# Local attention on one Trainium2 core: the mask written by eight small products instead of two full-size ones

## The reference, cut to what matters

```python
DEPTH, HEADS, DIM_HEAD, WINDOW, QK_SCALE = 6, 16, 64, 32, 8.0
def local_attention(q, k, v):          # b, h, n=128, d=64
    nw = n // WINDOW                   # 4 blocks of 32 queries
    bq, bk, bv = (t.reshape(b, h, nw, WINDOW, d) for t in (q, k, v))
    def look(t):                       # keys: the block before, and the own block
        p = jnp.pad(t, ((0, 0), (0, 0), (1, 0), (0, 0), (0, 0)))
        return jnp.concatenate([p[:, :, :nw], p[:, :, 1:]], axis=3)
    bk2, bv2 = look(bk), look(bv)      # 64 keys for each block
    mask = (it < jb) | (it > jb + WINDOW) | (jb == -1)
    sim = jnp.einsum('bhwie,bhwje->bhwij', bq, bk2) * QK_SCALE
    sim = jnp.where(mask, -jnp.finfo(sim.dtype).max, sim)
    attn = jax.nn.softmax(sim, -1)
    return jnp.einsum('bhwij,bhwje->bhwie', attn, bv2)
```

## Time and profile before

| | |
|---|---|
| median of 3 runs | 2673.61 us (2669.58 to 2676.61) |
| the profiled execution: its time | 2672.38 us |
| its span | 2670.5 us |
| busy: PE | 2441.2 us, 91% |
| busy: DVE, ACT, POOL | 79%, 71%, 67% |
| granted clock of PE, mean of the span | 0.989 |

### The profile page before, as it was taken

One profiled execution on the slowest core, in us unless ns is written; L12 is line 12 of the kernel. 1 busy time (PEld: TensorE's weight loads), 2 busy tenths in 40 slices (PEclk: granted clock), 3 DMA queues, 4 the chain that ended last, 5 costly groups with the idle time before them and its releaser, 6 DMA issues.

```text
span 2670.5 us, 98096 instructions
## 1 busy us (share of the span) xinstructions
PE 2441.2 (91%) x36165; PEld 1693.3 (63%) x36169; DVE 2098.9 (79%) x4531; ACT 1896.1 (71%) x6651; POOL 1781.0 (67%) x1605
## 2 busy tenths in 40 slices
PE   6989877778999999999999999999999999889999
PEld 3656644446666666666666666666666666558884
DVE  6777789987888888888888888888888888665544
ACT  3666688867787778878877887887788878543323
POOL 1566787649878778777778787787777777512210
PEclk8999999999999999999999999999999999989999
DMA  5000020021111211121112111121112111100000
GB/s 138 11 10 11 11 49 13 12 66 33 34 31 39 56 40 32 31 64 40 32 32 55 40 40 32 45 52 40 31 33 63 40 33 32 40 1 1 1 1 16
DMA packets 177424, 92.28 MB, mean 35 GB/s; under 512 B 40950, under 2 KB 173256, under 8 KB 176976
## 3 DMA queue, kind: packets, MB, share of 16 engines
q1 hardware_dynamic: 168352, 82.00, 12.0%
q0 software_dynamic: 8192, 4.21, 1.2%
q10 hardware_dynamic: 432, 0.07, 0.0%
HBM read 32.06 MB, written 3.76 MB: 13 GB/s over the span
## 4 chain that ended last, share of the span: by engine, by line
POOL 34%; PE 21%; issue 11%; DVE 7%; ACT 3%; DMA 1%; SPq 1%; DVEq 0%; POOLq 0%; ACTq 0%
POOL rs L1505 16%; POOL t_pair L1495 12%; POOL pr L1486 5%; PE bank L1113 2%; PE scores L1158 2%; PE bank L1169 2%; PE bank L1106 1%; PE bank L1797 1%; PE bank L1821 1%; ACT pr L1428 1%; PE scores L1140 1%; PE bank L1198 1%; PE bank L2054 1%; DMA rg_prod<-vt 1%; PE bank L1791 1%
## 5 line engine op out<-in xcount | busy, mean ns | idle before, releaser
L1505 POOL TENSOR_TENSOR rs<-ssc,neg_half 128x8 f32<-128x8 f32 x384 | 645.9, 1682 | 30.4 <-DVE ssc L1376 30.4
L1495 POOL TENSOR_TENSOR t_pair<-qn_pair,tabs 128x512 f32<-128x512 f32 x384 | 488.7, 1273 | 12.7 <-DVE qn_pair L1360 9.9
L1428 ACT ACTIVATE pr<-scores,negmax 128x64 f32<-128x64 f32 x1536 | 462.1, 317 | 3.9
L1486 POOL TENSOR_TENSOR pr<-pr,rec 128x256 f32<-128x256 f32 x384 | 235.1, 612 | 333.2 <-DVE rec L1353 333.2
L1106 PE MATMUL bank<-wqk,xs 128*128 128x512 f32 x768 | 396.0, 598 | 4.8 <-DVE qn_pair L1360 3.6
L1422 ACT COPY vt<-bank 128x256 f32<-128x256 f32 x361 | 134.4, 372 | 281.2 <-PE bank L1169 243.8
L1428 ACT ACTIVATION_READ_ACCUMULATOR pr<-scores,negmax 128x1 f32 x1536 | 321.1, 209 | 0.0
L1011 POOL DMA_INDIRECT rg_win<-rg_images,share_down x256 | 259.6, 1014 | 83.4 <-issue 55.5
L1113 PEld LDWEIGHTS bank<-ident,qr_pair 128*128 128x128 f32 x1536 | 180.2, 142 | 180.2 <-DVE qr_pair L1340 143.2
L1360 DVE TENSOR_TENSOR qn_pair<-bank,rs 128x512 f32<-128x512 f32 x384 | 260.5, 678 | 20.0 <-POOL rs L1505 19.7
L1340 DVE TENSOR_TENSOR qr_pair<-t_pair 128x512 f32<-128x512 f32 x384 | 264.8, 690 | 10.7 <-issue 0.7
(11 more groups left out here) (309 smaller groups left out, 5505.4 us busy)
## 6 DMA issues: line engine op xcount, KB each, us to landing
rg_prod<-vt SPq DMA_DIRECT2D x1536, 32.0 KB
wqk<-in_L_ffn_Wqkv SPq DMA_DIRECT2D x20, 256.0 KB, 2.8
rg_win<-rg_images,share_down POOLq DMA_INDIRECT x256
wv<-in_L_ffn_Wqkv SPq DMA_DIRECT2D x20, 128.0 KB, 2.8
wo<-in_L_ffn_Wo SPq DMA_DIRECT2D x20, 128.0 KB
w<-in_L_ffn_W SPq DMA_DIRECT2D x6, 341.0 KB
rg_images<-rg_prod SPq DMA_DIRECT2D x1, 1625.0 KB, 7.9
rg_images<-XT SPq DMA_DIRECT2D x16, 64.0 KB, 1.5
```

Of the source, the lines that this page charges most:

```text
L1428: ex = act.activation(pr[t % 2][:, h * BAND:(h + 1) * BAND], sl_ps[:, h // 2, h % 2 * BAND:(h % 2 + 1) * BAND], ACT.Exp, bias=negmax[t % 2 ...
L1486: pool.tensor_tensor(p, p, over(rec[t % 2][:, :], [P, GH, BAND], 2), ALU.mult).then_inc(a.p_scaled, 1)
L1495: pool.tensor_tensor(t2[t % 2][:, :].rearrange("p (i h f e) -> p i h f e", i=2, h=GH, f=2), qn[t % 2][:, :].rearrange("p (i h f e) -> p i ...
L1505: pool.tensor_tensor(rs[t % 2][:, :], ssc[t % 2][:, :], neg_half[:, 0:8], ALU.pow)\
```

## The change

The mask is written in the tile shape of the scores: for each block of 32 queries and each half `r` of the rows one product, eight in all, each 64 rows by 32 columns with 128 moving columns. The operands change places. The stationary one is now a 64x32 piece of the mask, which is stored transposed (keys down, queries across) and twice, once for each half of the rows; the moving one is the 64x64 diagonal block of `ident16`, read twice for the two heads. A tile's mask has the same 32 rows and 128 columns of PSUM as its scores.

```diff
@@ build @@
-        local_mask = sb("local_mask", [P, BAND], BF16)
+        local_mask = sb("local_mask", [P, P], BF16)
...
-        mask_wide, pick_wide = t1[0][:, 0:BAND], oT[1][0:ME, 0:ME * P]
+        mask_wide, pick_wide = t1[0][:, 0:P], oT[1][0:ME, 0:ME * P]
@@ score @@
-                for r in range(2):
-                    pe.matmul(sl_ps[:, r, :].rearrange("p (a k) -> p a k", a=2), ident16[:, :],
-                              over(local_mask[:, :], [P, 2, BAND], 1), start=True, stop=False, skip_group_check=True)
+                for _, lo in BLOCKS:
+                    for r in range(2):
+                        row = slice(r * HD, (r + 1) * HD)
+                        pe.matmul(sl_ps[lo:lo + WINDOW, r, :].rearrange("p (a k) -> p a k", a=2),
+                                  local_mask[row, lo:lo + WINDOW], over(ident16[row, row], [HD, 2, BAND], 1),
+                                  start=True, stop=False, skip_group_check=True)
@@ constants @@
-        "c_local_mask": np.where(band, 0.0, MASKED).astype(f),
+        "c_local_mask": np.tile(np.where(band, 0.0, MASKED).T, (2, 1)).astype(f),
```

## The result

The change made the kernel slower. Its median is 2690.65 us (2687.73 to 2694.91, six runs), against 2671.14 us (2669.58 to 2676.61, six runs) of the kernel before on the same chip: a ratio of 1.0070 with a 95% interval of 1.0057 to 1.0083. I had forecast 18 us less; it is 19.5 more. The profiled span is 2688.7 us against 2670.5, so 18.2 longer, and the local layers, from the first mask to the last, hold 13.2 of them.

The account below looks back on a forecast made before the run. PE was taken to bound the local layers: eleven slots at 0.055 us and one at 0.15 give 0.755 us a round, 18.1 us over 24 rounds, so a median of 2655.5 us, range 2646 to 2668.

Parts of the forecast that it names:

- What bounds the kernel: Local layers: PE, busy 96% of a round, is the only path in many slots; ACT and DVE wait for it.
- eleven slots of a round: Of a round's 16 masks, four are covered by ACT or POOL; eleven gain 0.055 us each, one 0.15.
- The mask's own terms: Each slot's mask: two full products, 0.11 us, go; one set of eight, 0.055 us, comes; 0.055 us less.
- the change of shape: PE's switch from 128x128 to 64x32: its 0.10 us stays but moves from between mask and scores to before the mask.
- rival on the mask: At the mask's eight products: poor overlap, about 2702 us, 8%; or exposed weights, 2663 us, 12%.
- exposed load: Rival at the mask's set: its weights are exposed, it costs 0.08 us, the gain falls to 11 us, 2663; 12%.
- The forecast's bound: Mask's set: not shorter than 0.047 us, the start of eight passes, so at most 0.063 us gained per slot.
- the slower rival: Mask's eight products don't overlap well, through a minimum distance between starts or a shared bank: about 2702 us, 8%.
- one more set in front of the four score sets: Start of the burst: the eight mask products cost one later score set, 0.055 us, with the scores' sets unchanged.
- My list of what would show me wrong: Mask to scores above 0.11 us, scores' sets beyond 0.23, or PE's waits growing as much as its slots shrink.
- the forecast of "slower": Whole kernel: 0.08 chance of slower, all for the mask's eight products not overlapping well, about 2702 us.
- The GELU's term: Mask behind the GELU's pause, once a round: 0.15 us less, 0.055 plus the 0.10 change of shape hidden in the wait.

Follow-up runs that it names:

- 12, 13, 14 scores: The changed kernel with only 12, 13 or 14 of a slot's 16 score products: 2669.81 us (0.9956 of the kernel before), 2676.88 and 2678.53 us.
- mask last: The changed kernel with its eight mask products behind the 16 scores instead of ahead of them: 2711.34 us, 1.0122 of the kernel before.
- six tiny products: The kernel before with six added 64x32 bf16 products of two moving columns behind its mask, into unused columns: 2713.01 us, kernel before 2676.86.
- two timed pairs: Change against kernel before on one chip: 2690.17 against 2675.04 us; both with two useless f32 products in the GELU's pause: 2681.73 against 2673.53.
- twelve scores: Two kernels without a slot's last four score products: the change with eight mask products 2669.81 us, the kernel before with two 2674.03.

## Why the prediction was wrong

**What bounds the kernel: right.** PE is the path in the slots, and PE's waits for ACT and DVE did not move (46.9 to 47.3 us, 24.7 to 25.5). That the slots' change reaches the end in eleven slots of a round was right as well: in eleven the distance from mask to mask grew by 0.030 to 0.032 us (medians over 17 rounds), the others sum to -0.04, and the round grew by 0.30.

**The mask's own terms: right.** The set of eight costs 0.066 us to the first score where I had said 0.08, and the change of shape moved in front of the mask as foreseen: 0.093 us more from transposes to mask (0.438 to 0.531), forecast 0.10 less rounding. Transposes to first score fell from 0.643 to 0.597, so by 0.046, near the 0.055 of the forecast, and what its rounded parts had given (0.44 - 0.395). The matmuls at the mask's line are the 3072 that were to be seen:

```profile
L1136 PEld LDWEIGHTS scores<-ident,local_mask x3072: 88/89/99, 601.2 to 2326.4; 64*32 64x32 bf16 x192
L1136 PE MATMUL scores<-ident,local_mask x3072: 212/227/287, 601.2 to 2326.4; 64*32 64x128 bf16 x192
```

Neither rival on the mask came true: eight starts take 0.023 us, so there is no least distance that shows, and no exposed load. The forecast's bound, that a set can't start in less than 0.047 us, was wrong, and changed nothing. The Trainium skill's floor of about 25 ns between starts ("TensorE: Matmul & The Clock Gate", section "Wait — 56ns, not 53.3ns?"), which stood behind the slower rival, is not seen between products in different tiles.

**The step that failed first** is the one that kept the scores as they were: "one more set in front of the four score sets", with the four sets' 0.23 us unchanged behind it. I costed streaming and weights of each set and never counted instructions. The burst of 68 before fits because its large mask products have ended in time; a burst of 80 behind eight small ones does not, and 68 behind eight small ones does not either. Score to attend took 0.077 us more, which turns -0.046 into +0.031 in each slot, a slot of 4.46 us against the 4.37 forecast (before 4.43), and 7 us. My list of what would show me wrong had this ("if scores' sets stretch beyond 0.23", here 0.32), but no rival had it, and the forecast of "slower" was tied to the mask's products alone. The runs show the mechanism from five sides (12, 13, 14 scores, mask last, six tiny products).

**The second failure** is a cost that I did not have at all: the clock. I read a granted clock of 1.00 in one round and took it as fixed. Behind the pause of 1.9 us it is not. In the two timed pairs the change costs 6.9 us (15.1 - 8.2) more when the pause is open, of which the mean clocks account for 2 to 4, and the rest stays open. Why the change brings more stretches is not settled: the profiled executions have 1 before, 5 and 6 with the change, 12 without a mask, 14 and 7 with twelve scores, 8 and 6 with 13 and 14, 10 with the mask last and 11 with the six tiny products. Neither more nor less work of PE orders this list. All that the runs show is that they go when the pause is filled.

**The GELU's term was mis-sized.** I had 0.15 us there, since the change of shape would hide in the pause. The distance from the mask before the pause to that behind it is 6.606 us, and was 6.611: ACT ends it, whatever PE does earlier, and each slot behind it still has one change of shape on its path. So the term is nothing instead of 0.15.

Of the 18.2 us of span, 13.2 lie in the local layers (by the profile 7 slots, 6 clock), 2.7 ahead of them and 2.2 behind; I have no experiment on these last five. Single profiled executions differ by as much: the change has 1725.21 us in the local layers in one and 1732.04 in the other. So the near match of 14.2 and 13.2 is partly luck. What carries the argument is the slot: score to `attend` is 0.460 or 0.461 us in all four profiles with eight mask products and 16 scores, and 0.384 in all four with two.

## What to carry to other kernels

When small tile products replace large ones, count instructions as well as columns: weight loads and matmuls between the last full drain and the end of the burst, against about 64, and look at the last products of the burst, not at the ones that were changed. Read the granted clock behind every pause of the engine over all rounds of a stage, and in the mean over all executions, not in one profile. Test a change with the pause filled, against the kernel before filled in the same way, before a difference is put down to the change's own work. And a gain on the busiest engine is spent by whoever comes second: without the mask PE waited 26 us more at `attend`.

## What the runs showed of the hardware

- In these bursts PE starts at most 64 instructions (loads and products together) past the oldest one that has not ended, and makes room in program order: the held product starts 0.026 to 0.027 us after the end of the product 64 places ahead of it, in three kernels. The 13th score product, instructions 65 to 68, costs 0.061 us where a whole set of eight passes starts in 0.05. The Trainium skill gives that depth, 64, as TensorE's queue and reorder window ("TensorE: Matmul & The Clock Gate", section "Architectural detail: the array is 16× 32×32, not 1× 128×128"); the trace agrees with the number.
- Small bf16 products in different tiles start 3.3 ns apart (0.023 us for eight). In the Trainium skill the same page, section "Measured speedup vs the span model", has about 4 ns for each tile; the trace agrees.
- A change from 128x128 to 64x32 costs 0.093 us between transposes and mask and 0.095 (0.205 - 0.11) between mask and scores, and nothing where PE waits anyway (6.606 us from mask to mask across the GELU's pause, before 6.611).
- Behind a wait of 0.93 to 1.94 us PE's clock was at times granted at 1.2 GHz for 3.4 us, 1 to 14 times in the local layers of one execution, at some 1.7 us each; most stood behind the GELU's pause. With 1.46 us of useless products in that pause and a wait of 0.64 us left, there was none in the profiles of all seven kernels with the filling.
